# Attention layer of a two-layer sequence kernel: x and half of the hidden blocks multiplied as plain fp32

## The reference

```
lam = exp(-exp(nu_log) + 1j * exp(theta_log));  gamma = sqrt(1 - |lam|^2)      # 32 states
Bu = x @ (gamma * (B_re + 1j * B_im)).T
states = scan over the 256 positions: s = lam * s + Bu
y = real(states @ (C_re + 1j * C_im).T) + x @ D_mat.T
z = gelu_tanh(y @ W1) @ W2                      # 128 -> 512 -> 128
x = layernorm(x + (x + sigmoid(res_logit) * z))

p = softmax(x @ Wg)                             # 8 experts, the 2 best of each token are used
out = sum over the 2: p_e * (gelu(x @ FW1[e] + fb1[e]) @ FW2[e] + fb2[e])
x = layernorm(x + out)
```

## Time and profile before

| engine | busy us | share of the span | instructions |
|---|---|---|---|
| PE (TensorE matmul) | 275.6 | 72% | 1329 |
| DVE (VectorE) | 278.8 | 72% | 791 |
| ACT (ScalarE) | 233.1 | 61% | 498 |
| POOL (GpSimd) | 226.1 | 59% | 281 |

### The profile page before, as it was taken

The page is one execution under the profiler, slowest core; times in us unless marked ns, Lnnn a source line. Parts: engine busy times, 40 slices in busy tenths (PEclk is TensorE's granted clock), DMA queues, the critical chain, the costliest instruction groups (busy, mean ns, idle before and its releaser), DMA issues.

```text
span 385.0 us, 5368 instructions
## 1 busy us (share of the span) xinstructions
PE 275.6 (72%) x1329; PEld 225.6 (59%) x1329; DVE 278.8 (72%) x791; ACT 233.1 (61%) x498; POOL 226.1 (59%) x281
## 2 busy tenths in 40 slices
PE   1467998699867739339643039999999999962940
PEld 1234776377535429239533029999999999941410
DVE  2999889999984978409931027999999999930680
ACT  2406665577753756508731037999999999950461
POOL 4888156638867767710677724666666766671460
PEclk9999999789979968958986558999999999995885
DMA  3633203101101122120222213222222222115732
GB/s 103 197 95 115 78 1 109 56 0 49 43 28 48 43 69 64 42 56 22 58 88 99 95 63 104 84 83 86 82 85 81 68 84 83 61 43 207 282 103 82
DMA packets 27189, 31.19 MB, mean 81 GB/s; under 512 B 4632, under 2 KB 22560, under 8 KB 27160
## 3 DMA queue, kind: packets, MB, share of 16 engines
q1 hardware_dynamic: 22328, 20.89, 18.0%
q0 software_dynamic: 4832, 9.97, 7.7%
HBM read 16.99 MB, written 13.86 MB: 80 GB/s over the span
## 4 chain that ended last, share of the span: by engine, by line
DVE 41%; issue 20%; PE 15%; POOL 9%; DMA 5%; ACT 4%; DVEq 1%; another core or an unknown queue 1%; SPq 1%; ACTq 0%; POOLq 0%
DVE h_l L928 8%; DVE wuse L891 7%; POOL slots_d L448 5%; DVE h_h L924 4%; PE bank L1028 3%; PE bank L1030 3%; PE bank L1029 3%; DVE work L693 2%; DVE h_l L697 2%; POOL results_d L454 2%; PE bank L1170 2%; PE bank L1178 1%; ACT fw L616 1%; DVE xt_l L914 1%; DMA late<-slots_d 1%
## 5 line engine op out<-in xcount | busy, mean ns | idle before, releaser
L454 POOL DMA_INDIRECT results_d<-work,dest x87 | 88.7, 1019 | 54.6 <-ACT work L590 34.1
L448 POOL DMA_INDIRECT slots_d<-rows,slot_i x64 | 66.6, 1040 | 38.6 <-DVE rows L830 19.4
L574 ACT ACTIVATE h<-bank,buse 128x384 f32<-128x384 f32 x116 | 67.8, 584 | 32.8 <-issue 21.5
L928 DVE TENSOR_TENSOR h_l<-h,h_h 128x384 fp32r<-128x384 f32 x116 | 64.5, 556 | 27.4 <-ACT h_h L579 23.6
L1028 PE MATMUL bank<-h_h,wuse 128*128 128x384 f32 (+1 forms) x148 | 60.5, 409 | 3.9 <-DVE h_l L697 1.6
L1028 PE MATMUL bank<-xt_h,wuse 128*128 128x384 f32 x116 | 42.2, 364 | 26.1 <-issue 20.2
L1029 PE MATMUL bank<-h_l,wuse 128*128 128x384 f32 (+1 forms) x148 | 53.3, 360 | 0.0
L1030 PE MATMUL bank<-h_h,wuse 128*128 128x384 f32 (+1 forms) x148 | 53.2, 360 | 0.0
L520 ACT ACTIVATE h<-bank 128x512 f32<-128x512 f32 x32 | 19.0, 595 | 38.3 <-DVE h_l L697 18.8
L891 DVE CAST wuse<-fw 128x1024 fp32r x58 | 40.0, 691 | 1.4 <-issue 1.4
L1029 PE MATMUL bank<-xt_l,wuse 128*128 128x384 f32 x116 | 40.8, 352 | 0.0
(11 more groups left out here) (213 smaller groups left out, 610.4 us busy)
## 6 DMA issues: line engine op xcount, KB each, us to landing
late<-slots_d SPq DMA_DIRECT2D x29, 195.0 KB
late<-in_L_ffn_W_dram SPq DMA_DIRECT2D x16, 256.0 KB, 2.8
work<-in_L_attn_x3d_dram SPq DMA_DIRECT2D x8, 256.0 KB, 3.3
rows<-results_d SPq DMA_DIRECT2D x4, 512.0 KB, 5.1
work<-results_d SPq DMA_DIRECT2D x4, 512.0 KB, 8.5
out_dram<-fw SPq DMA_DIRECT2D x8, 256.0 KB, 2.3
slots_d<-zeros SPq DMA_DIRECT2D x9, 195.0 KB, 4.1
results_d<-work,dest POOLq DMA_INDIRECT x87
```

The costliest lines, as they stand in the source:

```text
L448: pool.indirect_dma_start(out=slots_d, out_offset=bass.IndirectOffsetOnAxis(ap=slot_i[:, k, i:i + 1], axis=0), in_=rows[:, k, i, :], in_of ...
L454: pool.indirect_dma_start(out=results_d, out_offset=bass.IndirectOffsetOnAxis(ap=dest[:, SQ * g + q:SQ * g + q + 1], axis=0), in_=yo[:, g ...
L574: act.activation(h32[:, b % 2, 0:SLOTS], H_PS[b % 2][:, 0:SLOTS], ACT.Gelu, bias=buse[:, k, b:b + 1]).then_inc(sm["gelu_b"], 1)
L928: dve.tensor_tensor(ht_l[b], h32[:, b % 2, 0:SLOTS], ht_h[b].bitcast(F32), ALU.subtract).then_inc(sm["hbl_ready"], 1)
```

## The change

x, and the last two of the four hidden blocks, are no longer split: `xt32` goes into the B and the D product as it is, and ACT's gelu writes hidden blocks 2 and 3 straight to an fp32 tile `h_fp`, which is multiplied by W2 as it was loaded. The weights B, D and the cosine and sine weights are copied from PSUM in one instruction. On PE the D product is put ahead of the wait for the states. `turn_back` is one instruction over both tables. `route_choice(g, 1)` and `route_hits(g)` move from the head of chunk c to chunk c - 1, behind `turn_in`.

```
+SPLIT = 2
...
-        bt_h, bt_l = sb("bt_h", [P, P], F32R), sb("bt_l", [P, P], F32R)
-        dt_h, dt_l = sb("dt_h", [P, P], F32R), sb("dt_l", [P, P], F32R)
-        wcs = sb("wcs", [P, 2, P])
+        setw = sb("setw", [P, 4 * P])
+        bt, dt, wcs_re, wcs_im = (setw[:, n * P:(n + 1) * P] for n in range(4))
...
+        qcs = work[:, 2 * CHUNK:4 * CHUNK].rearrange("p (n a s) -> p n a s", n=2, a=2)
...
+        h_fp = sb("h_fp", [P, HB - SPLIT, CHUNK])
...
-                act.copy(xt32[:, c % 3, :], XT_PS[:])
-                wait(act, sm["y_ready"], c - 1)
-                act.copy(xt_h[:, c % 2, :], XT_PS[:]).then_inc(sm["xt_sb"], 1)
+                act.copy(xt32[:, c % 3, :], XT_PS[:]).then_inc(sm["xt_sb"], 1)
...
-                    wait(act, sm["hl_ready"], n - 1)
-                    act.activation(h32[:, b % 2, :], H_PS[b % 2][:], ACT.Gelu_apprx_tanh).then_inc(sm["h_act"], 1)
-                    act.wait_ge(sm["h_act"], n + 1)
-                    wait(act, sm["z_ready"], n + 1 - HB)
-                    act.copy(h_h[:, b, :], h32[:, b % 2, :]).then_inc(sm["hh_ready"], 1)
+                    if b < SPLIT:
+                        wait(act, sm["hl_ready"], SPLIT * (c - 1) + b + 1)
+                        act.activation(h32[:, b, :], H_PS[b % 2][:], ACT.Gelu_apprx_tanh).then_inc(sm["h_act"], 1)
+                        act.wait_ge(sm["h_act"], n + 1)
+                        wait(act, sm["z_ready"], n + 1 - HB)
+                        act.copy(h_h[:, b, :], h32[:, b, :]).then_inc(sm["hh_ready"], 1)
+                    else:
+                        wait(act, sm["z_ready"], n + 1 - HB)
+                        act.activation(h_fp[:, b - SPLIT, :], H_PS[b % 2][:], ACT.Gelu_apprx_tanh).then_inc(sm["h_act"], 1)
...
-            dve.tensor_copy(bt_h[:], Z_PS[:, 0:P])
-            dve.tensor_copy(dt_h[:], Z_PS[:, P:2 * P])
-            link(dve.tensor_copy(wcs[:, :, :].rearrange("p a n -> p (a n)"), Z_PS[:, 2 * P:4 * P]))
-            dve.tensor_tensor(bt_l[:], Z_PS[:, 0:P], bt_h[:].bitcast(F32), ALU.subtract)
-            dve.tensor_tensor(dt_l[:], Z_PS[:, P:2 * P], dt_h[:].bitcast(F32), ALU.subtract).then_inc(sm["setup_sb"], 1)
-            def x_split(c):
-                dve.wait_ge(sm["xt_sb"], c + 1)
-                dve.tensor_tensor(xt_l[:, c % 2, :], xt32[:, c % 3, :], xt_h[:, c % 2, :].bitcast(F32), ALU.subtract).then_inc(sm["x_lo"], 1)
+            dve.tensor_copy(setw[:], Z_PS[:]).then_inc(sm["setup_sb"], 1)
 
             dve.wait_ge(sm["cs_ready"], 1)
-            x_split(0)
...
-            def turn_back(c, n):
+            def turn_back(c):
 
                 dve.wait_ge(sm["u_ready"], c + 1)
                 wait(dve, sm["y_ready"], c)
-                dve.tensor_tensor(two((qc, qs)[n]), two(ut), both(cs[:, n, :]), ALU.mult).then_inc(sm["q_ready"], 1)
+                dve.tensor_tensor(qcs, ut.rearrange("p (n a s) -> p n a s", n=1, a=2).to_broadcast([P, 2, 2, S]),
+                                  cs[:, :, :].rearrange("p n (a s) -> p n a s", a=1).to_broadcast([P, 2, 2, S]), ALU.mult).then_inc(sm["q_ready"], 1)
 
             def hidden_low(c, b):
-                dve.wait_ge(sm["hh_ready"], HB * c + b + 1)
-                dve.tensor_tensor(h_l[:, b, :], h32[:, b % 2, :], h_h[:, b, :].bitcast(F32), ALU.subtract).then_inc(sm["hl_ready"], 1)
+                dve.wait_ge(sm["hh_ready"], SPLIT * c + b + 1)
+                dve.tensor_tensor(h_l[:, b, :], h32[:, b, :], h_h[:, b, :].bitcast(F32), ALU.subtract).then_inc(sm["hl_ready"], 1)
...
-                    turn_back(c + 1, 0)
-                    turn_back(c + 1, 1)
+                    turn_back(c + 1)
                 if routing:
-                    route_choice(g, 1)
-                    route_hits(g)
                     logits(c - 1)
                 hidden_low(c, 0)
                 hidden_low(c, 1)
                 if routing:
                     route_ranks(g)
                     route_slots(g)
-                if c + 2 < NCH:
-                    x_split(c + 2)
-                hidden_low(c, 2)
                 if c >= 1 and not routing:
                     logits(c - 1)
-                hidden_low(c, 3)
...
+                if c + 1 in ROUTING:
+                    route_choice(ROUTING[c + 1], 1)
+                    route_hits(ROUTING[c + 1])
...
-            turn_back(0, 0)
-            turn_back(0, 1)
-            x_split(1)
+            turn_back(0)
 
             dve.wait_ge(sm["aw_loaded"], 32)
+            part = SPLIT * D
             dve.tensor_copy(w1_h, aw_st[:, 0, :])
-            link(dve.tensor_copy(w2_h, aw_st[:, 1, :]))
+            link(dve.tensor_copy(w2_h[:, 0:part], aw_st[:, 1, 0:part]))
             dve.tensor_tensor(w1_l, aw_st[:, 0, :], w1_h.bitcast(F32), ALU.subtract)
-            dve.tensor_tensor(w2_l, aw_st[:, 1, :], w2_h.bitcast(F32), ALU.subtract).then_inc(sm["w_ready"], 1)
+            dve.tensor_tensor(w2_l[:, 0:part], aw_st[:, 1, 0:part], w2_h[:, 0:part].bitcast(F32), ALU.subtract).then_inc(sm["w_ready"], 1)
...
-                pe.wait_ge(sm["x_lo"], c + 1)
+                pe.wait_ge(sm["xt_sb"], c + 1)
                 wait(pe, sm["p_ready"], c)
-                products(BU_PS[:], bt_h[:], bt_l[:], xt_h[:, c % 2, :], xt_l[:, c % 2, :], True, True).then_inc(sm["bu_ready"], 1)
+                mm(BU_PS[:], bt, xt32[:, c % 3, :], start=True, stop=True).then_inc(sm["bu_ready"], 1)
...
-                pe.wait_ge(sm["q_ready"], 2 * c + 2)
-                mm(Y_PS[:], wcs[:, 0, :], qc, start=True, stop=False)
-                mm(Y_PS[:], wcs[:, 1, :], qs, start=False, stop=False)
-                products(Y_PS[:], dt_h[:], dt_l[:], xt_h[:, c % 2, :], xt_l[:, c % 2, :], False, True).then_inc(sm["y_ready"], 1)
+                mm(Y_PS[:], dt, xt32[:, c % 3, :], start=True, stop=False)
+                pe.wait_ge(sm["q_ready"], c + 1)
+                mm(Y_PS[:], wcs_re, qc, start=False, stop=False)
+                mm(Y_PS[:], wcs_im, qs, start=False, stop=True).then_inc(sm["y_ready"], 1)
...
-                    pe.wait_ge(sm["hl_ready"], HB * c + b + 1)
-                    products(Z_PS[:], w2_h[:, b * D:(b + 1) * D], w2_l[:, b * D:(b + 1) * D], h_h[:, b, :], h_l[:, b, :],
-                             b == 0, b == HB - 1).then_inc(sm["z_ready"], 1)
+                    if b < SPLIT:
+                        pe.wait_ge(sm["hl_ready"], SPLIT * c + b + 1)
+                        products(Z_PS[:], w2_h[:, b * D:(b + 1) * D], w2_l[:, b * D:(b + 1) * D], h_h[:, b, :], h_l[:, b, :],
+                                 b == 0, b == HB - 1).then_inc(sm["z_ready"], 1)
+                    else:
+                        pe.wait_ge(sm["h_act"], HB * c + b + 1)
+                        mm(Z_PS[:], aw_st[:, 1, b * D:(b + 1) * D], h_fp[:, b - SPLIT, :], start=b == 0, stop=b == HB - 1).then_inc(sm["z_ready"], 1)
```

More of the change, by code:

```diff
@@ L161, in build @@
         yo = work[:, 0:YO * SLOTS].rearrange("p (m q d) -> p m q d", m=YO, q=SQ)
-        xt_h, xt_l = sb("xt_h", [P, 2, CHUNK], F32R), sb("xt_l", [P, 2, CHUNK], F32R)
+        xt_h, xt_l = sb("xt_h", [P, 2, SLOTS], F32R), sb("xt_l", [P, 2, SLOTS], F32R)
         y_h, y_l = sb("y_h", [P, CHUNK], F32R), sb("y_l", [P, CHUNK], F32R)
         h32 = sb("h32", [P, 2, CHUNK])
+        h_fp = sb("h_fp", [P, HB - SPLIT, CHUNK])
         h_h, h_l = sb("h_h", [P, HB, CHUNK], F32R), sb("h_l", [P, HB, CHUNK], F32R)
@@ L205, in build @@
         xb = late[:, 4 * CHUNK - 2 * SQ * ROW:].rearrange("p (k q r) -> p k q r", k=2, q=SQ)
-        xbt_h = [xt_h[:, k, 0:SLOTS] for k in range(2)]
-        xbt_l = [xt_l[:, k, 0:SLOTS] for k in range(2)]
+        xbt_h = [xt_h[:, k, :] for k in range(2)]
+        xbt_l = [xt_l[:, k, :] for k in range(2)]
         yt = rt
@@ L234, in build @@
             tables_ready cc_ready setup_t setup_sb w_ready wgm_ready wgc_ready fw_hi fw_lo
-            xT_ready xt_sb x_lo bu_ready p_ready u_ready q_ready y_ready y_hi y_lo
+            xT_ready xt_sb bu_ready p_ready u_ready q_ready y_ready y_hi y_lo
             pre_a h_act hh_ready hl_ready z_ready r_ready st_ready mv_ready ve_ready rstd_ready nmr_ready
```

## The result

Four runs of the changed kernel have a median of 365.26 us (360.71 to 367.91), beside 371.91 for the kernel before on the same chip: ratio 0.9721, interval 0.967 to 0.9773. Six later runs on another chip have 364.68 (361.82 to 366.73) beside 372.54: 0.9792, interval 0.9738 to 0.9845. Both intervals lie under 1. So the gain is 7 to 10 us; the prediction was 363.1, a gain of 9.0. A run over 1.5% above the fastest of its kernel counts as disturbed and is left out of every ratio, which is why a ratio needn't equal that of the medians. The profiled execution has a span of 365.8 us.

What follows compares the result with a forecast made beforehand. Attention's chain to chunk 2's aggregate, then POOL's row scatters, was taken to bound the kernel. Chunk 2's aggregate 7.0 us earlier and 2.0 of POOL idle gone took 372.06 to 363.1 us, range 358.5 to 368.5.

Steps and rivals of the forecast that it cites:

- Plain products: On PE, each of four plain fp32 products a chunk costs +0.15 us, +0.6 in all: period 11.05 where PE binds.
- Splits removed on DVE: On DVE, one x split and two hidden splits go per chunk, 0.6 us each, 1.8 a chunk.
- One product instruction: On DVE, one cosine and sine instruction instead of two saves nearly nothing, 0.05 us; the page's estimate was 0.16.
- Start and chunk 0: Setup and first chunk: turn-back of chunk 1 2.8 us earlier, at 28.2; residual sum of chunk 0 4.0 earlier, at 37.1.
- Moved choice: On DVE, routing moved ahead of chunk 2's residual sum adds 2.26 us there; that sum comes at 62.5, 1.1 earlier.
- Chunk 3: DVE without pause takes 11.4 us instead of 17.24; residual sum at 73.9, 7.0 us earlier.
- POOL: POOL's scatters: chunk 2's norm at 75.9, the 2.02 us idle before chunk 4's norm goes; 9.0 us gained at their end.
- From profile to runs: The profile's 9.0 us gain carries over unscaled to the timed runs, 372.06 to 363.1, though the profile is 12.9 longer.
- PE at 1.2 GHz for half of attention: Slower rival: half of PE's work from 36.7 to 73.9 us runs at half clock, time 379.7 us; chance 0.07.
- smaller-gain case: Rival: PE at half clock in chunk 3 ends z 3.1 us after DVE, time 366.2 us; chance 0.17.
- larger gain: Rival: the other routing of chunks 2 and 3 also loses its stretch, another 2.4 us, time 360.7; chance 0.09.
- hid the gain: Rival: something behind 139 us not tied to tile 0 sets the end, time 372 us; chance 0.07.

Runs made afterwards that it cites:

- experiment 8: The changed kernel plus one spare POOL fill ahead of each expert tile's scatters; median 372.83 us, ratio 1.0049 to the kernel before.
- experiment 9: The changed kernel plus four spare linked VectorE products ahead of chunk 3's residual sum; median 373.02 us, ratio 0.9928 to the kernel before.
- experiments 9 and 10: The changed kernel with four spare VectorE products before chunk 3's residual sum (ratio 0.9928), and with ten spare PE matmuls before chunk 2's logits (0.9744).
- the second profile of before: The kernel before, run and profiled again unchanged; median 372.54 us, profiled span 371.9 us.
- experiment 4: The changed kernel with all four hidden blocks plain, none split; median 361.38 us, ratio 0.9691 to the kernel before.
- experiment 1: The changed kernel run again unchanged; median 364.68 us, ratio 0.9792 to the kernel before.
- experiment 6: The changed kernel with the cosine and sine products as two VectorE instructions again; median 363.99 us, ratio 0.983 to the kernel before.

## Why the prediction was right

The mechanism held: attention gives POOL's first scatters an earlier start, and the rest hangs on POOL. Step by step:

- *Plain products.* Period 11.05 forecast, 11.11 measured (45.84 to 56.95), 0.86 each at full clock. Right.
- *Splits removed on DVE.* 0.6 each forecast; two still there take 1.21 start to start (49.43 to 50.64). Right.
- *One product instruction.* 0.05 forecast, 0.07 measured; 0.16, the estimate from the Trainium skill's page "VectorE: DVE Perf Modes" (section "The TRN2 errata — SBUF-src ops pay a fixed extra latency per instruction"), is not what the runs show. Beside POOL's weight splitting it took 2.29 (at 36.14).
- *Start and chunk 0.* -2.8 forecast for the turn-back of chunk 1, -3.88 measured (27.10): in the second stretch 1.0 went and not 1.7, but instructions that I had left as they were took 1.7 less. The turn-back itself then took 1.13 to the next start, where I had kept the stretched 2.7 of the pair in the earlier trace rows. Residual sum of chunk 0 35.50, not 37.1. Too small, and partly by chance: experiments 8 and 9, with the same code up to there, have that sum at 36.59 and 36.61.
- *Moved choice.* 2.26 forecast, 2.24 measured (59.57 to 61.81); residual sum of chunk 2 at 61.81 for 62.5. Right, with luck in the sum: chunk 0 was 1.6 early, and the scan ahead of the choice took 2.34 for 1.62.
- *Chunk 3.* This term was mis-sized: 11.4 forecast "without pause", 13.47 measured. DVE pauses 2.90 for the ranks, which stand behind the logits and three plain products in PE's order. I priced PE's lateness at the end of z, where it had room (73.56, the residual sum at 75.28), and not at the ranks. At full clock the wait is 1.25 (experiments 9 and 10) and chunk 3 takes 1.2 less, so 1.2 us of the miss are the half clock; the other 0.9 I put down to the order. The sum is -5.6, not -7.0.
- *POOL.* The idle before the norm of chunk 4 went, as forecast; norm to norm took 26.46 for 25.73, since the norm of chunk 3 took 3.30 for 2.21 up to its first scatter (its first instruction 0.72 for 0.22). First tile load 131.34 for 129.7: -7.4 of -9.0. The wait of the norm of chunk 7 is 3.81, forecast about 3.
- *From profile to runs.* First tile load to the end took 234.5 us, 246.3 before: the difference is inside the 12.9 that I allowed, and the second profile of before, without the hole of 18.8 us, has 233.5. Carrying the gain over unscaled was right. That the time met the forecast better than the first tile load did is chance: two profiles of the changed kernel differ by 2.8 us behind it.

The rivals. PE at 1.2 GHz for half of attention didn't come: 36 to 58 us has PE full at 1.00. With the Trainium skill's page "TensorE: Matmul & The Clock Gate" (Part 1), by which the throttled state is the default and activity lifts it, the trace agrees there. The smaller-gain case, half clock in chunk 3, did come: the sign that I had named, a clock below 0.9 before 75 us, is there (0.74 and 0.84), but it acted through the ranks and not at the end of z, at a price of 1.2 instead of 3.1. The larger gain did not: the rest of the routing that I had hoped to see freed took 5.95 us for 5.91. Nothing behind the first tile load hid the gain.

By parts, each from one profile taken out of or put into a whole: x plain 3.5 us of the norm, two hidden blocks plain 3.6, the moved choice 0.2. The single product instruction appears to cost 0.8; its own rows save 0.07, and the two profiles differ by the clock in chunk 3, which can move each of these figures by some 1.2.

## What to carry to other kernels

Price a shorter engine at each wait of its partner, not only at the end of the stage: a step moved up on DVE gave PE a wait, and PE's later results came back to DVE as a wait in the next stage. Where one engine issues a chain of transfers, find the first and the last instruction in attention that it waits for; a gain at the first counts only as far as the later ones keep up (experiment 4: 1.7 of 2.6). And compare two profiles of the same kernel before reading a hole in one as a cost.

## What the runs showed of the hardware

The same instructions up to chunk 3, with the same PE wait of 2.50 us, had a clock of 1.00 in one execution (experiment 9) and 0.75 and 0.83 in another, on another chip (experiment 8). Scatters that POOL issues to send results back take 0.95 to 1.69 us each (experiment 1) with no cause in the profile, and their mean differs by 37 ns between two executions of the changed kernel, 3.2 us over 87 of them. Four linked DVE products of 512 take 0.98 each (experiment 9), unlinked ones 0.6 (experiment 6).
